# Chunk 0 of k in two fp16 parts: a DMA transpose and three fp16 products in M, in a fused attention and feed-forward kernel

## What is computed

```python
xn = layernorm(x)                                   # over the 1024
q = Wq @ xn;  k = Wk @ c;  v = Wv @ c               # 512 x 1024, heads of 64 rows
q = softmax(q, axis=d) * 64 ** -0.5                 # over the 64 rows of a head
k = softmax(k, axis=n)                              # over the 1024 tokens
context = einsum('bhdn,bhen->bhde', k, v)
out = einsum('bhde,bhdn->bhen', context, q)
out = Wo @ out + bo;  out = out / norm(out) * g * sqrt(128)
x = x + out
x = x + layernorm(x) @ dequant(qweight, scales, zeros) + bias
```

## Time and profile before

| | us |
|---|---|
| median of 3 runs (lowest to highest) | 672.92 (672.76 to 673.13) |
| the profiled execution | 670.46 |
| its span, from the first to the last instruction | 668.7 |
| PE busy, share of the span | 633.6, 95% |
| DVE busy | 550.3, 82% |
| POOL busy | 468.5, 70% |
| ACT busy | 455.1, 68% |
| PEld busy | 385.1, 58% |
| matmuls of M (`ps_m`, L1224), busy | 119.1 |
| transposes of k (L1208), busy | 39.2 and 39.0 |
| share of PE in the chain that ended last | 83% |

### The profile page before, as it was taken

How to read it: one execution, slowest core, us unless ns; L and a number is a source line. 1 busy time by engine, 2 the same in 40 slices (tenths; PEclk the granted TensorE clock), 3 DMA queues, 4 the chain that set the end, 5 groups by cost and what they waited for, 6 DMA issues and landing times.

```text
span 668.7 us, 10173 instructions
## 1 busy us (share of the span) xinstructions
PE 633.6 (95%) x3285; PEld 385.1 (58%) x3302; DVE 550.3 (82%) x897; ACT 455.1 (68%) x741; POOL 468.5 (70%) x409
## 2 busy tenths in 40 slices
...
GB/s 304 43 121 79 93 57 94 190 96 153 84 132 116 93 181 96 189 63 154 84 96 172 96 190 72 157 80 108 153 95 190 94 144 87 117 65 94 111 143 63
DMA packets 179236, 79.35 MB, mean 119 GB/s; under 512 B 168536, under 2 KB 170096, under 8 KB 179184
## 3 DMA queue, kind: packets, MB, share of 16 engines
...
...
## 4 chain that ended last, share of the span: by engine, by line
PE 83%; DVE 6%; ACT 3%; POOL 3%; issue 2%; DMA 1%; another core or an unknown queue 0%; SPq 0%; POOLq 0%; DVEq 0%; ACTq 0%
PE ps_m L1224 14%; PE ps_m L1319 14%; PE ps_k L1154 5%; PE ps_ta L1208 4%; PE ps_k L1155 4%; PE ps_k L1156 4%; PE ps_q L1154 4%; PE ps_q L1156 4%; PE ps_q L1155 4%; PE ps_tb L1208 4%; PE ps_o L1156 4%; PE ps_o L1154 4%; PE ps_o L1155 4%; PE ps_o L1419 4%; PE ps_o L1237 2%
## 5 line engine op out<-in xcount | busy, mean ns | idle before, releaser
L457 POOL TENSOR_TENSOR q_tok_lo<-q_exp,q_tok_hi 128x1024 f16<-128x1024 f32 x64 | 137.7, 2153 | 90.0 <-ACT q_tok_hi L611 88.4
L430 POOL TENSOR_TENSOR q_exp<-q_exp,q_rec 128x1024 f32<-128x1024 f32 x64 | 121.7, 1902 | 5.0
L586 ACT ACTIVATE k_exp<-ps_k,k_nmax 128x1024 f32<-128x1024 f32 x64 | 71.0, 1109 | 76.7 <-DVE k_nmax L858 76.7
L1224 PE MATMUL ps_m<-k_t,c_t 128*128 128x512 f32 x256 | 119.1, 599 | 0.0
L600 ACT ACTIVATE q_exp<-q_exp,w_unit 128x512 f32<-128x512 f32 x128 | 92.0, 720 | 39.0 <-DVE q_exp L870 39.0
L865 DVE TENSOR_REDUCE q_nmax<-ps_q 128x8 f32<-128x512 f32 x128 | 87.7, 685 | 27.6 <-PE ps_q L1156 27.2
L858 DVE TENSOR_REDUCE k_nmax<-ps_k 128x1 f32<-128x1024 f32 x64 | 77.3, 1208 | 19.7 <-PE ps_k L1156 19.7
L870 DVE TENSOR_TENSOR q_exp<-ps_q,q_nmax 128x512 f32<-128x512 f32 x128 | 88.5, 692 | 4.4
L611 ACT ACTIVATE q_tok_hi<-q_exp 128x1024 f16<-128x1024 f32 x64 | 67.5, 1055 | 23.6 <-POOL q_exp L430 23.6
L877 DVE TENSOR_REDUCE q_sum<-q_exp 128x16 f32<-128x1024 f32 x64 | 77.3, 1209 | 0.9 <-ACT q_exp L600 0.8
L1154 PE MATMUL ps_k<-c_hi,wk_lo 128*128 128x512 f32 x128 | 67.5, 527 | 3.3 <-ACT k_exp L586 3.2
...
## 6 DMA issues: line engine op xcount, KB each, us to landing
...
q_hi<-q_tok_hi SPq DMA_TRANSPOSE x64, 3.1
q_lo<-q_tok_lo SPq DMA_TRANSPOSE x64, 3.2
```

The costliest lines, as they stand in the source:

```text
L430: nc.gpsimd.tensor_tensor(pair, pair, rec.unsqueeze(2).to_broadcast([P, 2 * HEADS, DH]), ALU.mult).then_inc(qs_done, 1)
L457: nc.gpsimd.tensor_tensor(q_tok_lo[p % 2][:], q_exp[:, 2 * p:2 * p + 2, :].rearrange("p t d -> p (t d)"), q_tok_hi[p % 2][:], ALU.subtract ...
L1224: last = nc.tensor.matmul(ps_m[:], c_t[s][:, t, :], k_t[:, t, :], start=(t == 0), stop=(t == TC - 1))
```

## The change

- Chunk 0 of k (`TURNED = 1`) isn't transposed by TensorE. ScalarE copies its exponential to fp16 (`high_k`), GpSimd subtracts (`low_k`), and SyncE transposes both parts by DMA (`turn_k`) into `k_t_hi` and `k_t_lo`. Chunks 1 to 3 go on as before, one step j later; `k_t` has three chunks.
- So that the parts fit fp16, chunk 0's exponent gets ln(2^12) added: a small ScalarE step makes `k_bias` ahead of `exp_k(0)`.
- c transposed is scaled by `c_fit` (range 2^12). `move_tc` writes it twice, to fp16 (`c_t_hi`) and fp32 (`c_t`); VectorE's `low_tc` makes `c_t_lo`. `fit_c` (two small steps) makes the factor; `g_fit` is now a constant of the set-up, and `fit_g` becomes `undo_g` with two steps.
- In `mix_m` the first 128 columns are three fp16 products, the other 384 one fp32 product.
- `split_rs` goes from ScalarE to GpSimd in passes 2 to 15. `low_x2` goes from j = 0 to j = 1 on VectorE. On SyncE `x2_lo` goes ahead of the hi part of pair 3, and `turn_k` behind its lo part.
- Some tiles now share memory with others (the weights' landing place is `q_exp` in place of `k_t`; `x2n_hi` and `x2n_lo` lie in `spare`, whose name later rows bear; `g_hi` and `g_lo` lie in `g_parts`).

```diff
...
+            def turn_k(b, j):
+
+                for tok, turned, done, turned_sem in ((k_hi, k_t_hi, khi_done, khi_turned),
+                                                      (k_lo, k_t_lo, klo_done, klo_turned)):
+                    sp.wait_ge(done, TURNED * b + j + 1)
+                    if b > 0:
+                        sp.wait_ge(m_ready, b)
+                    sp.dma_start_transpose(turned[:, :, j * P:(j + 1) * P], tok[j][:]).then_inc(turned_sem, 16)
...
                 if do_c:
                     turn_q(c, 2, "lo")
-                    turn_q(c, 3, "hi")
                 if do_f:
                     sp.wait_ge(x2lo_done, f + 1)
...
                 if do_c:
+                    turn_q(c, 3, "hi")
                     turn_q(c, 3, "lo")
                 if do_a:
+                    for j in range(TURNED):
+                        turn_k(a, j)
...
+                def low_k(j):
+
+                    pool.wait_ge(khi_done, TURNED * a + j + 1)
+                    if begun(a):
+                        pool.wait_ge(klo_turned, 16 * TURNED * a)
+                    nc.gpsimd.tensor_tensor(k_lo[j][:], k_exp[:, j, :], k_hi[j][:], ALU.subtract).then_inc(klo_done, 1)
...
                 def exp_k(b, sums, j):
                     act.wait_ge(kmax_done, 4 * b + j + 1)
-                    if begun(8 * b + 2 * (j - 2) + 2):
-                        act.wait_ge(tk_ready, 8 * b + 2 * (j - 2) + 2)
-                    nc.scalar.activation(k_exp[:, j % 2, :], ps_k[:], ACT.Exp, bias=k_nmax[:, j:j + 1],
+                    bias = k_nmax[:, j:j + 1]
+                    if j < TURNED:
+                        if begun(b):
+                            act.wait_ge(kexp_done, 4 * (b - 1) + j + 1)
+                        nc.scalar.activation(k_bias[:, j:j + 1], bias, ACT.Identity,
+                                             bias=k_lift[:]).then_inc(kbias_done, 1)
+                        act.wait_ge(kbias_done, TURNED * b + j + 1)
+                        bias = k_bias[:, j:j + 1]
+                    held, of = (j - 2, b) if j >= 2 else (j + 2, b - 1)
+                    if of >= 0:
+                        if held < TURNED:
+                            act.wait_ge(klo_done, TURNED * of + held + 1)
+                        else:
+                            act.wait_ge(tk_ready, TK * of + 2 * (held - TURNED) + 2)
+                    nc.scalar.activation(k_exp[:, j % 2, :], ps_k[:], ACT.Exp, bias=bias,
                                          accum_out=k_sum[:, sums, j:j + 1]).then_inc(kexp_done, 1)
...
+                    nc.scalar.activation(c_t_hi[1 - s][:, 4 * h:4 * h + 4, :], turned, ACT.Identity,
+                                         scale=c_fit[:]).then_inc(cthi_done, 1)
+                    nc.scalar.activation(c_t[1 - s][:, 4 * h:4 * h + 4, :], turned, ACT.Identity,
+                                         scale=c_fit[:]).then_inc(tc_moved, 1)
...
                         high_x2()
-                        split_rs(f, rs2)
                     if j == 0 and do_a:
+                        high_k(0)
                         exp_k(a, s, 1)
...
+                def low_tc(b, sb_, h):
+
+                    dve.wait_ge(tc_moved, 2 * b + h + 1)
+                    nc.vector.scalar_tensor_tensor(out=c_t_lo[sb_][:, 4 * h:4 * h + 4, :].rearrange("p t c -> p (t c)"),
+                                                   in0=(ps_ta, ps_tb)[h][:], scalar=c_fit[:],
+                                                   in1=c_t_hi[sb_][:, 4 * h:4 * h + 4, :].rearrange("p t c -> p (t c)"),
+                                                   op0=ALU.mult, op1=ALU.subtract).then_inc(ctlo_done, 1)
...
+                        if j == 1 and TURNED == 1:
+                            low_tc(a, s, 1)
+                        if j == 1 and do_f:
+                            low_x2(f)
                         max_k(a, j + 1)
...
-                    if j == 0 and do_f:
-                        low_x2(f)
...
-                        last = nc.tensor.matmul(ps_m[:], c_t[s][:, t, :], k_t[:, t, :], start=(t == 0),
+                        three(ps_m[:, 0:TURNED * P], c_t_hi[s][:, t, :], c_t_lo[s][:, t, :], k_t_hi[:, t, :],
+                              k_t_lo[:, t, :], start=(t == 0), stop=False)
+                        last = nc.tensor.matmul(ps_m[:, TURNED * P:], c_t[s][:, t, :], k_t[:, t, :], start=False,
                                                 stop=(t == TC - 1))
...
-                    if 1 <= j < 5 and do_a:
-                        transpose_k(2 * (j - 1))
+                    if TURNED < j < 5 and do_a:
+                        transpose_k(2 * (j - 1 - TURNED))
```

More of the change, by code:

```diff
@@ L109, in build @@
         c_t = [sb(f"c_t{s}", [P, TC, P]) for s in range(2)]
+        c_t_hi = [sb(f"c_t_hi{s}", [P, TC, P], F16) for s in range(2)]
+        c_t_lo = [sb(f"c_t_lo{s}", [P, TC, P], F16) for s in range(2)]
+        c_unit = sb("c_unit", [P, 1])
+        c_fit = sb("c_fit", [P, 1])
+        g_back = sb("g_back", [P, 1])
+        gs_back = sb("gs_back", [P, 1])
         c_abs = sb("c_abs", [P, 1])
@@ L129, in build @@
         k_rec = sb("k_rec", [P, HC])
-        k_t = sb("k_t", [P, TC, HID])
+        k_lift = sb("k_lift", [P, 1])
+        k_bias = sb("k_bias", [P, TURNED])
+        k_hi = [sb(f"k_hi{j}", [P, N], F16) for j in range(TURNED)]
+        k_lo = [sb(f"k_lo{j}", [P, N], F16) for j in range(TURNED)]
+        k_t_hi = sb("k_t_hi", [P, TC, TURNED * P], F16)
+        k_t_lo = sb("k_t_lo", [P, TC, TURNED * P], F16)
+        k_t = sb("k_t", [P, TC, HID - TURNED * P])
         q_tok_hi = [sb(f"q_tok_hi{r}", [P, 2 * HID], F16) for r in range(2)]
```

182 lines of the change are left out of this document (125 added, 57 removed).

## The result

The changed kernel takes **694.59 us** (median; 692.7 to 697.15), the kernel before 673.02 on the same chip: a ratio of 1.0315, 95% interval 1.0273 to 1.0357. It is slower, as forecast, but by 21.6 us and not by 3.5, and outside the range. The sequence of rival 2 is what happened. The profiled execution took 695.4, its span is 693.6.

The account below looks back on a forecast made before the run. TensorE bounds the pass; -0.87 us of work, 1.0 idle and 0.11 for project_k(3) give +0.25, +3.3 over thirteen passes. With +0.5 at the start, 670.46 becomes 674.3; adding the median's 2.5 gives 676.7, said as 676.5; range 671.5 to 692.

Parts of the forecast that it names:

- rival 2: Shared SBUF read path: low_k reads before x2n_lo, making project_k(3) 1.34 us later a pass; 690.5 us; chance 0.16.
- The bound, and that the saving is not given back: Steady pass: TensorE bounds it, but its saved 0.87 us goes into idling before mix_out(0) and project_k(2).
- TensorE's work: Steady pass: eight transposes fewer save 0.87 us; mix_m steps stay at 0.86, so no gain there.
- `k_bias`: ScalarE ahead of exp_k(0): adds 0.32 us, so exp_k(1) ends 0.27 later and delays project_k(2).
- The failed step: who reads first: VectorE against GpSimd: x2n_lo asks just ahead of low_k, which is stretched by 1.0 us; project_k(3) loses 0.11 more.
- The forecast's own case: Whole kernel: steady pass of 38.7 to 38.9 us, 676.5 us in all, own range 673.5 to 679.5; chance 0.55.
- Rival 3: mix_m: fp16 products of 128 columns take 0.11 us, not 0.05; up to 0.48 a pass more, 683.5 us; chance 0.10.
- The start: Ahead of the steady passes: k_bias and the second c_t copy delay project_k(1) by 0.5 us, ends -1 to +2.
- The DMA transposes at nothing: SyncE's queue: two further DMA transposes a pass cost nothing, being read over 5 us after their issue.

Follow-up runs that it names:

- e1: The changed kernel with VectorE's x2n_lo issued ahead of the second low_tc, not behind it; 678.3 us against 672.19, ratio 1.0094.
- e4: The changed kernel with x2n_lo ahead of the second low_tc and without k_bias; 671.61 us against 672.19, ratio 1.0002.
- e5: The kernel before with six of the eight transposes of k's chunk 0 left out; 669.35 us against 670.36, ratio 0.9983.
- e2: The changed kernel without k_bias, so chunk 0 is not scaled up by 4096; 690.04 us, ratio 1.0269.
- e10: The kernel before with x2n_lo moved behind the q shift of j = 1; 670.66 us against 671.03, ratio 0.9991.

## Why the prediction was wrong

The pass in pieces, from the start of one TensorE matmul to the start of another, in us, means of twelve steady passes:

| | before | changed | e1 | e4 |
|---|---|---|---|---|
| `project_q(0)` and the first half of `project_k(1)` | 1.44 | 1.63 | 1.63 | 1.44 |
| the second half of `project_k(1)`, `project_q(1)`, the transposes around it | 2.32 | 2.13 | 2.13 | 2.13 |
| the first half of the feed-forward and `project_k(3)` | 3.12 | 4.36 | 3.19 | 3.13 |
| from the first product of `mix_m` to the end of the pass | 10.24 | 10.31 | 10.31 | 10.31 |
| all the rest | 21.43 | 21.41 | 21.40 | 21.42 |
| the pass | 38.55 | 39.84 | 38.66 | 38.43 |

- **The bound, and that the saving is not given back: right.** e5 shows it alone (0.65 us of work gone, 0.06 gained). Two followers were named, `exp_k(1)` and `g_lo`. It is `g_lo` that TensorE waits for; `project_k(2)` follows `mix_out(0)` without an idle mark.
- **TensorE's work: right within a tenth.** The transposes took 0.87 with them, and `mix_m` with what stands between its products costs 0.07 more: 0.80 less. Of this, 0.68 is lost again in front of `mix_out(0)` (2.13 for 2.32 - 0.87 = 1.45).
- **`k_bias`: the duration right, its way to TensorE wrong.** It was to make `exp_k(1)` 0.27 later. Counted from `project_q(0)`, `exp_k(1)` starts at 5.91 in both kernels (296.23 - 290.32, 305.35 - 299.44). TensorE pays in a place that the forecast left out, `project_k(1)`, whose load waits for `exp_k(0)` (the idle mark at 300.17): 0.19 a pass in the changed kernel and in e1, nothing in e4. By e2, `k_bias` costs 0.24 in all, not 0.32.
- **The failed step: who reads first.** The forecast had `x2n_lo` ask at 297.86 to 297.94 "just ahead of" `low_k` at 297.97 to 298.1, so that `k_nmax` of chunk 2 would wait for TensorE only and `exp_k(2)` cost 0.11. What happened is the other order: `k_lo` asked 0.16 first, `x2n_lo` stood for 1.83, and `exp_k(2)` costs TensorE 1.24 in front of `project_k(3)` (4.36 for 3.12), nearly the whole of the 1.28. Counted from the pass's first q shift (291.17), the forecast was 6.69 to 6.77 for `x2n_lo` and 6.80 to 6.93 for `k_lo`; measured, 6.86 and 6.69. VectorE was 0.09 to 0.17 late: `k_bias` delays `m_t`, `mix_g` and with it `g_hi` (idle 0.56 in front, for TensorE's `ps_o`), which I had left out of VectorE's time. In e2, without `k_bias`, `x2n_lo` asks at 6.67. GpSimd was 0.11 to 0.24 early, most of it because `q_tok_lo` came 0.19 later than before and not 0.32. Each error is a tenth or two of a microsecond. I had worked out a margin of 0.03 to 0.24, and given the other side of it 0.16; with errors of this size it deserved about a half.
- **Rival 2 was right in its mechanism, and nearly in its price**: `x2n_lo` 3.3 (3.06), `k_lo` 2.15 (2.15), the pass 1.34 longer (1.28). Its 690.5 is 4 us short of the result; in the profiled execution the start is 2.3 and the end 5.5 us longer, for which it had nothing. The forecast's own case, had it come, is nearly e1: 38.66 a pass and 678.3, against 38.8 and 676.5. That the sizes are so near is in part luck. The forecast made them up of `exp_k(1)` (0.14) and `k_lo` (0.11); in e1 they are `exp_k(0)` (0.19), `k_lo` and `mix_m` (0.07 each), less 0.19 that is left of the saving in front of `mix_out(0)`.
- **Rival 3 (products of 128 columns at 0.11): wrong.** They start 0.05 to 0.06 apart. The Trainium skill (TensorE: Matmul & The Clock Gate, "Back-to-back issue gap") gives 81 ns for it; the rows above have 55, and the measurement decides.
- **The start: open.** It was 2.3 us longer, for +0.5 forecast. But the kernel before and e10 have the same program up to there and differ by 1.3 us (19.3 and 18.1), e5 by 2.1 the other way (21.4): a single profile can't say.
- The DMA transposes at nothing: nothing in the trace of after contradicts it; no steady wait for `turn_k` shows.
